# A two-layer graph network on one core: the mixers' output products folded, the second mixer moved between the edge tiles, the table stage reordered

## The reference, cut to what matters

```python
edge_index = jnp.stack([src, dst])
xn = _layernorm(x)
x = x + _L0_gnn_ref(xn, edge_index, ...) + _L0_mix_ref(xn[None], ...)[0]
x = x + _L0_ffn_ref(_layernorm(x)[None], ...)[0]          # top 2 of 8 experts
xn = _layernorm(x)
x = x + _L1_gnn_ref(xn, edge_attr_4, edge_attr_32, edge_index, ...) + _L1_mix_ref(xn[None], ...)[0]
x = x + _L1_ffn_ref(_layernorm(x)[None], ...)[0]          # one of 16 experts

def _L1_mix_ref(x, W_qkv, W_proj, b_proj):                # 8 heads of 64
    q, k, v = split(x @ W_qkv.T)
    q_, k_ = relu(q) + scale, relu(k) + scale
    kv, k_sum = einsum('bnhe,bnhf->bhef', k_, v), sum(k_, axis=nodes)
    z = 1.0 / (einsum('bnhe,bhe->bnh', q_, k_sum) + EPS)
    out = einsum('bnhe,bhef->bnhf', q_, kv) * z[..., None]
    return out.reshape(B, N, C) @ W_proj.T + b_proj

def _L1_gnn_ref(...):                                     # per edge e from node s to node d
    w = ssp(edge_attr @ W_f1) @ W_f2 * (ssp(s0(d, s) @ W_s1) @ W_s2)      # 512 weights of the edge
    edge_feat = w combined with x[s] and edge_sh          # 512 features
    out = segment_sum(edge_feat, edge_dst) + self_x       # then a linear map, + x
```

## Time and profile before

| | |
|---|---|
| profiled execution, its time | 5409.32 us |
| its span, first to last instruction | 5407.2 us |
| PE, DVE, POOL, ACT busy (share of the span) | 85%, 68%, 57%, 38% |
| mean granted TensorE clock | 0.922 of full speed |
| moved by DMA | 894.86 MB, mean 165 GB/s |

### The profile page before, as it was taken

How to read it: one execution, slowest core, us unless ns; L and a number is a source line. 1 busy time by engine, 2 the same in 40 slices (tenths; PEclk the granted TensorE clock), 3 DMA queues, 4 the chain that set the end, 5 groups by cost and what they waited for, 6 DMA issues and landing times. The chain is left out here.

```text
span 5407.2 us, 69046 instructions
## 1 busy us (share of the span) xinstructions
PE 4589.8 (85%) x17435; PEld 2475.2 (46%) x17436; DVE 3697.7 (68%) x9349; ACT 2077.3 (38%) x4487; POOL 3062.4 (57%) x2740
## 2 busy tenths in 40 slices
PE   6889988886999899597789888888888888888797
PEld 3346633232555555465556544443343343343463
DVE  6622279998999833324754488888888887878554
ACT  1112222222333211132300166666666666666310
POOL 0677767776777620123320288888888888888200
PEclk9999989998999999698899898899989998989898
DMA  4241157776666611644543499998888998988634
GB/s 148 77 145 44 44 168 210 210 210 166 193 196 194 187 40 52 228 129 139 176 156 129 148 202 205 203 206 200 201 202 199 204 203 195 203 199 200 162 104 144
DMA packets 363058, 894.86 MB, mean 165 GB/s; under 512 B 87037, under 2 KB 110188, under 8 KB 359205
## 3 DMA queue, kind: packets, MB, share of 16 engines
q0 software_dynamic: 212464, 648.99, 49.2%
q1 hardware_dynamic: 131151, 201.88, 11.1%
q10 hardware_dynamic: 19190, 41.03, 2.0%
HBM read 670.91 MB, written 221.22 MB: 165 GB/s over the span
## 5 line engine op out<-in xcount | busy, mean ns | idle before, releaser
L2028 POOL DMA_INDIRECT mid_acc<-m_out,m_il x416 | 703.8, 1692 | 142.1 <-issue 114.7
L2016 POOL DMA_INDIRECT m_drow<-mid_drow,m_ig x416 | 460.1, 1106 | 425.4 <-DMA m_ig<-in_dst_ix 290.1
L2240 PE MATMUL m_pws<-m_w,m_hid 32*128 32x512 f32 x832 | 499.8, 682 | 207.0 <-DVE m_hid L2070 180.0
L2248 PE MATMUL m_pm<-m_msg,m_same 128*128 128x512 f32 x832 | 528.3, 720 | 102.7 <-DVE m_msg L2107 64.2
L961 PE MATMUL m_pm<-m_vrow,m_same 128*128 128x512 f32 x880 | 513.5, 669 | 80.8 <-DVE m_vrow L904 79.5
L433 POOL DMA_INDIRECT mid_slots<-sort_rec,f_row x416 | 413.6, 994 | 246.5 <-issue 126.5
L888 POOL DMA_INDIRECT m_vrow<-mid_att_rows,m_ix x440 | 431.1, 980 | 167.9 <-PE m_pm L962 86.3
L2211 PEld LDWEIGHTS m_pip<-keep_ident,m_drow 128*128 128x128 f32 x2496 | 399.2, 219 | 255.3 <-issue 245.0
L2241 PE MATMUL m_pwf<-m_w,m_hid 32*128 32x512 f32 x832 | 507.4, 692 | 0.0
L735 POOL DMA_INDIRECT s_krow<-mid_att_rows,s_ix x440 | 416.0, 946 | 146.8 <-issue 123.1
L2016 POOL DMA_INDIRECT m_srow<-mid_srow,m_ig x416 | 425.9, 1024 | 126.8 <-issue 119.2
(11 more groups left out here) (386 smaller groups left out, 8981.0 us busy)
## 6 DMA issues: line engine op xcount, KB each, us to landing
x_line<-in_src_rows SPq DMA_DIRECT2D x26, 1024.0 KB, 5.2
mid_att_rows<-f_rows SPq DMA_DIRECT2D x75, 256.0 KB, 2.0
mid_ys<-e_y SPq DMA_DIRECT2D x57, 256.0 KB, 2.0
mid_acc<-e_zero ACTq DMA_DIRECT2D x26, 512.0 KB, 8.1
g_q<-mid_qT SPq DMA_DIRECT2D x50, 256.0 KB, 4.4
g_a<-mid_acc SPq DMA_DIRECT2D x50, 256.0 KB, 2.9
mid_srow<-t_srow SPq DMA_DIRECT2D x5, 2240.0 KB, 7.3
keep_w<-in_w SPq DMA_DIRECT2D x16, 512.0 KB, 8.9
```

Source lines behind the costliest of these rows:

```text
L2016: pool.indirect_dma_start(row, None, table, bass.IndirectOffsetOnAxis(ap=ig[:, k // EH, n, k % EH:k % EH + 1], axis=0),).then_inc(s_g[k % ...
L2028: pool.indirect_dma_start(io["acc1"][k % NACC], bass.IndirectOffsetOnAxis(ap=il[:, k // EH, k % EH:k % EH + 1], axis=0), out[:, k % R, :], ...
L2240: pe.matmul(pws[k % 2][:], hid[0:HID, par, cols], w_2[0:HID, :], start=True, stop=True)
L2248: pe.matmul(pm[:], same[:, k // B % 2, k % B, :], msg[:, k % 2, :], start=True, stop=True).then_inc(s_seg, 1)
```

## The change: what it does

- **Folded mixers.** In merge0 and merge1 kv is multiplied by the output weights once (kvw, 4 matmuls of 128x512 after a turn of kv). Per tile q is divided by its normalizer: ksum is now 128 columns wide, so that PE (`head_sums`) gives the normalizer of every column, ACT adds the epsilon (`normalizers`), VectorE takes the reciprocal of 128x512 and multiplies q by it, and PE multiplies q by kvw. The products with 2 columns, the turn of the result and ACT's copy of it are gone. In merge1 both output biases come in by a matmul with two rows (`two`, `extra`), and own rows are no longer loaded nor added.
- **front0.** keys and three of five member steps run ahead of the first tile; all later steps of the sort stand four places earlier. k'v and k'1 are one product with 129 columns.
- **load_consts, experts0.** One index table fewer is loaded, and the bf16 lines are no longer made. Only one accumulator and the last 128 rows of the other are cleared (14 DMAs for 26). The counts, with 52 broadcasts of 512 KB that GpSimd issues, and the lead rows are made in experts0.
- **tables1.** xT has two buffers; norms, turns and square sums of a pass stand in the middle of the pass before; ACT squares and adds the residual in place of VectorE and GpSimd; the hidden products stand ahead of the destination rows. srow's first part is stored from drow, and the node's own rows are stored to srow and once more to the accumulator acc1[0].
- **mixer1 and leads1 are gone.** In edges1 the blocks 1 to 25 each take one node tile of the mixer. The target numbers come as 512 KB broadcasts into SBUF instead of 4 KB rows and a matmul, and the ring of source rows has 12 slots.

```diff
@@ front0: order(k)
-                    if k == 0:
-                        keys()
-                    elif k < 1 + U:
-                        member(k - 1)
-                    elif k < 19:
-                        rank(2 * (k - 6))
+                    if k < 2:
+                        member(3 + k)
+                    elif k < 15:
+                        rank(2 * (k - 2))
...
-                    elif k == 22:
+                    elif k == 18:
                         bases(pcnt[:, 0:NT], pcnt[:, NT:2 * NT])
-                    elif 23 <= k < 23 + 2 * SORT_C:
+                    elif 19 <= k < 19 + 2 * SORT_C:
...
                 norms(0)
+                norms(1)
+                keys()
+                for a in range(3):
+                    member(a)
                 vec.wait_ge(s_bias, 16)
@@ merge0 (merge1 alike)
+                def divide_queries(i, j):
                     n = U * i + j
+                    vec.wait_ge(s_zq, n + 1)
+                    vec.reciprocal(zq[:, n % 2, :], zq[:, n % 2, :]).then_inc(s_rq, 1)
+                    vec.wait_ge(s_rq, n + 1)
+                    vec.tensor_tensor(q[:, j, :], q[:, j, :], zq[:, n % 2, :], ALU.mult).then_inc(s_q, 1)
...
+                for c in range(KC):
+                    need(pe, s_kvw, c - 1)
+                    pe.matmul(pk[c % 2][:], kvT[:, P * c:P * (c + 1)], w_out[:, c, :], start=True, stop=True).then_inc(s_kw, 1)
...
-                            pe.matmul(pout[j % 2][:], oT[:, j, P * c:P * (c + 1)], w_out[:, c, :], start=c == 0, stop=False)
+                            ins = pe.matmul(pout[n % 2][:], q[:, j, P * c:P * (c + 1)], kvw[:, c, :], start=False, stop=c == KC - 1)
@@ experts0: VectorE, with lines(b) on GpSimd for each half block
                 for n in range(XS + 2):
                     if n < XS:
                         first(n)
+                    if n < 2 * EB:
+                        counts(n, 0)
                     if n >= 2:
                         second(n - 2)
+                    if n < 2 * EB:
+                        counts(n, 1)
+                    if n == 2 * EB:
+                        vec.wait_ge(s_cnt, ET)
+                        lead_rows(vec, s_lead, keep.src, count, spare, go, leads)
@@ tables1: PE
+                turns(0)
...
                 for i in range(NB):
-                    body(i)
+                    scalars(i)
+                    hidden(i)
+                    destinations(i)
+                    gates(i)
+                    if i + 1 < NB:
+                        turns(i + 1)
+                    sources(i)
@@ edges1
-        S, R, B = EU, 4, 4
+        S, R, B = 12, 4, 4
...
-                        sp.dma_start(line[:, h, :], lines[:, cols]).then_inc(s_line[h], 16)
+                        mine = sources[(2 * b + h) * EH * P:(2 * b + h + 1) * EH * P].partition_broadcast(P)
+                        sp.dma_start(line[:, h].rearrange("p t n -> p (t n)"), mine).then_inc(s_line[h], 16)
+                        if h == 1:
+                            node(b)
...
+                def mixer(b, k):                       # PE, last in the body of edge tile k
...
+                    if k in (0, 1, 2, 3):
...
+                        for c in range(KC):
+                            ins = pe.matmul(px[:, P * k:P * (k + 1)], W[:, c, P * k:P * (k + 1)], xT[:, P * c:P * (c + 1)],
+                                            start=c == 0, stop=c == KC - 1)
+                    elif k in (5, 6, 7, 8):
...
+                        ins = pe.matmul(px[:], xT[:, P * c:P * (c + 1)], W[:, c, D:2 * D], start=c == 0, stop=c == KC - 1)
+                    elif k in (9, 10, 11, 12):
...
+                        ins = pe.matmul(px[:], xT[:, P * c:P * (c + 1)], W[:, c, 2 * D:3 * D], start=c == 0, stop=c == KC - 1)
+                    elif k == 14:
...
+                        for c in range(3):
+                            ins = pe.matmul(px[:, (P + 1) * c:(P + 1) * (c + 1)], key[:, P * c:P * (c + 1)], val[:, c, :],
+                                            start=True, stop=True)
+                    elif k == 15:
...
+                        ins = pe.matmul(px[:, 0:P + 1], key[:, 3 * P:D], val[:, 3, :], start=True, stop=True)
@@ program
-            run(mixer1)
-            run(leads1)
             run(edges1)
```

More of the change, by code:

```diff
@@ L1407, in experts0 @@
         zero = s.sb("zero", [P, 2 * D])
+        count, lower, spare = s.sb("count", [P, ET]), s.sb("lower", [P, P]), s.sb("spare", [P, 1])
+        line, junk = s.sb("line", [P, 2, EH, P], I32), s.sb("junk", [P, 2, P])
+        go, leads = s.sb("go", [P, 2, ET]), s.sb("leads", [P, ET], I32)
+        s_low, s_cnt, s_lead, s_lead_out = (s.sem(n) for n in ("lower", "counts", "lead_steps", "leads_out"))
+        s_line = [s.sem(f"line{k}") for k in range(2)]
         s_zero, s_z = s.sem("zero"), s.sem("sums_cleared")
@@ new lines, in norms, with residuals @@
+                def norms(i):
+                    act.wait_ge(s_sum, 2 * (i + 1))
+                    need(act, s_g1, 4 * i)
+                    act.activation(n1[:], sq[:, 0, :], ACT.Sqrt, scale=1.0 / 3.0).then_inc(s_n1, 1)
+                def residuals(i):
+                    act.wait_ge(s_v, NORM * (i + 1))
+                    for j in range(U):
+                        n = U * i + j
+                        act.wait_ge(s_xn, n + 1)
+                        act.activation(keep.X[:, n, :], keep.X[:, n, :], ACT.Identity, bias=resid[:, 1, n:n + 1],
+                                       scale=resid[:, 0, n:n + 1]).then_inc(s_res, 1)
@@ L2265, in body @@
                             inner(*there)
-                        if k % B == 0 and (there := at(b, k + B)):
-                            spread(*there)
                         if k % B == 1 and (there := at(b, k + 3)):
                             hidden(*there)
+                        mixer(b, k)
                 for b in range(EB):
@@ L2389, in _ @@
-                edges(0, 0)
-                mixed(0, 0)
-                pe.wait_ge(s_w, 48)
+                turn_kv(pe, keep.kv, keep.ident, pk[1]).then_inc(s_kv, 1)
+                sums(0, 0)
+                turn(0, 0)
+                pe.wait_ge(s_w, 64)
+                pe.wait_ge(s_two, 1)
+                pe.wait_ge(s_kvT, 1)
+                for c in range(KC):
+                    need(pe, s_kvw, c - 1)
+                    pe.matmul(pk[c % 2][:], kvT[:, P * c:P * (c + 1)], w_p[:, c, :], start=True, stop=True).then_inc(s_kw, 1)
```

830 lines of the change are left out of this document (399 added, 431 removed).

## The result

The changed kernel takes 5136.0 us (median of four runs, 5127.2 to 5150.2); beside it the kernel before took 5405.4. The ratio is 0.9508, with a 95% interval of 0.9493 to 0.9523. The forecast was 5012 in a range of 4965 to 5115: the direction was right, the time lies outside the range.

A forecast was written before the change was run, and what follows sets the result against it. GpSimd's issuing was taken to bound edges1. Terms −329.5 (mixer1, leads1), +32 (edges1), −19 (front0), −25 (merge0), −5 (merge1), −12 (experts0), −35 (tables1), −0.5 (load_consts) sum to −394: 5409.3 to 5015.3, less 3.6 gives 5012, range 4965 to 5115.

The forecast's parts named there:

- What bounds the kernel now: Reading of stage limits: edges1 is GpSimd's, 4.72 us per tile of issuing and gaps, times 416 = 1964 us.
- edges1, PE: PE has 68.3 us of full-clock work per block, 75.9 at 0.90, under GpSimd's 77.2; 31 us charged, bound +130.
- edges1, the ring: In edges1, 12 slots for 16 bind only when landings pass 12 us: cost nothing.
- edges1, DMA: In edges1, added mixer and line traffic of 129 us raises the DMA share from 0.89 to 0.94.
- +32: Whole edges1 term: 31 us for PE's narrow margin and 1 for the start; bounds −5 to +130.
- Rival 1: PE becomes the limit in edges1, +130 instead of +32: 5110 us; chance 0.17.
- rival 5: In edges1, VectorE's compare with two SBUF inputs stalls GpSimd, 110 us in all: 5122 at most; chance 0.03.
- front0: Stage front0: first scatter near 134 instead of 153.2, GpSimd's and PE's ends both earlier: −19 us, bounds 0 to −28.
- merge0: Stage merge0: 1.25 us less per tile on PE, about +5 for folding kv: −25 us, bounds −31 to +10.
- merge1: Stage merge1: tile from 6.95 to 6.57 us on PE, two-row bias product 0.87: −5 us, bounds −10 to +12.
- rival 6: Reciprocal of 512 columns takes 4.3 us or more, making merge1 VectorE's, +6 instead of −5: 5023 us; chance 0.08.
- experts0, tables1: experts0: 12 fewer clearing DMAs −15.4, counts' line loads +3, together −12 us; tables1: blocks near 31 us, −35 us.

The follow-up runs named there:

- no_products: Changed kernel without the mixer's arithmetic in edges1, its loads of xT, stores of q and the lines kept: 5169.5 us, edges1 2187.
- before_ring12: Kernel before with a ring of 12 source rows instead of 16 in edges1, nothing else: ratio to before 0.9998, edges1 2004.6 us against 2006.1.
- lines_once: Changed kernel with edges1's 512 KB target-number broadcasts issued for block 0 alone (2 of 52): 5036.4 us, edges1 2067.
- bare12: Changed kernel without the mixer's arithmetic, xT loads and q stores in edges1, lines for block 0 alone: edges1 2007.7 us, ratio to before 0.935.
- one_input: Changed kernel with each four-tile compare written as four instructions with one SBUF input and one number per partition: 5149.3 us, edges1 2184.
- line_pool: Changed kernel with edges1's 512 KB lines issued by GpSimd on its own queue instead of by SP: 5083.7 us, edges1 2118.
- before_lines_pool: Kernel before plus 52 unread 512 KB broadcasts in edges1, issued by GpSimd on its own queue: edges1 2082 us, ratio to before 1.012.

## Why the prediction was wrong, step by step

- **What bounds the kernel now**: right. edges1 was and stays GpSimd's; 0.30 us lie between its instructions as before. One row was misread on the way: the 290.1 us put down to an index load are not many gaps of 0.30 us but one wait of 290.1 us, ahead of the first gather and almost all of it before the stage. The sum of 4.72 us per tile doesn't use it.
- **edges1, PE**: the work was right. Forecast 68.3 us of full-clock work per block; 1893.0/26 × 0.92 = 67.0. But the 31 us charged for it measured nothing, and the +130 bound was built on PE as the limit: no_products excludes both.
- **edges1, the ring**: right (before_ring12).
- **edges1, DMA: the step that failed.** The prediction added SP's transfers to the mean share of the DMA engines, got 0.94 of the stage, and costed them at nothing as long as that stayed under 1. Their own size was right, 129 us per engine forecast and 134 measured. But it took GpSimd's 1.692, 1.106 and 1.024 us as fixed. They are not: they became 1.846, 1.164 and 1.155, and the share fell to 0.85 in a longer stage. The term "+32" measured +169: 108 lines, 59 xT and q (lines_once, bare12, no_products).
- **Rival 1** (PE) and **rival 5** (the shared port) were excluded by no_products and one_input; no rival had the mechanism that happened. Without it the sum is good: everything outside edges1 was forecast at −426 and came to −436 (5409.3 − 5141.95 is 267.4, and 169 were lost).
- **front0**: the first scatter starts at 132.2 (134 forecast), and the last ones follow each other by 1.26 us to the end, so GpSimd sets the stage's end as argued.
- **merge0**: −29.9, its mechanism right. **merge1**: a tile takes 6.90 us against 6.95, not 6.57, all of it on PE, which waits for nobody. The product with two rows costs nearly what the rest saved (1.05 for 1.10 us):

```profile
4838.49 1.05 PE L2460 MATMUL g_pout<-g_w_o,g_aT 128*128 128x128 f32 x8
4839.38 1.06 PE L978 MATMUL g_pn<-g_q,keep_ksum 128*128 128x128 f32 x8
4840.27 0.60 PE L2430 MATMUL g_tpa<-keep_ident,g_a 128*128 128x128 f32 x4
4840.80 1.12 PE L2451 MATMUL g_pout<-g_extra,g_two 2*128 2x512 f32 x2
4841.85 3.70 PE L2456 MATMUL g_pout<-g_kvw,g_q 128*128 128x512 f32 x8
4845.39 1.05 PE L2460 MATMUL g_pout<-g_w_o,g_aT 128*128 128x128 f32 x8
```

  From 4840.80 to 4841.85 the bias product takes 1.05 us, not 0.87, and what left the tile is 6.95 + 1.05 − 6.90 = 1.10 us, not 1.25.
- **The reciprocal** (rival 6): it was 3.35 us, nearer to the slope of the earlier trace rows (3.5) than to the 4.3 estimated from the Trainium skill, "VectorE: DVE Perf Modes", section "First, the fixed hardware budget". The measurement decides:

```profile
L2350 DVE RECIPROCAL g_zq<-g_zq 128x512 f32<-128x512 f32 x25 | 83.6, 3346 | 0.7 <-ACT g_zq L2392 0.7
```

- **experts0, tables1**: within 2 us (12 × 1.27 is 15.2, not the 15.4 of the sum). ACT's second copy waits 17.09 us instead of 32.95:

```profile
2204.32 0.60 ACT L1497 ACTIVATE e_xT<-e_tp 128x512 f32<-128x512 f32 x1 [17.09 <-issue]
```

## What to carry to other kernels

Where GpSimd's indirect DMAs set the pace, their issue times are not constants: transfers that SP issues lengthened them here at a mean DMA share of 0.85, though the engines were full for some 16 us after a load. The price was 4.1 to 4.5 us of stage per MB (108 us for 26 MB of lines, 59 for 13 MB of xT and q), and 6.0 in the kernel before (163 for 27 MB). Cost added transfers there by such a measured price, and try to issue them from GpSimd's list as well as making them smaller; on one chip either brought 56 to 60 us. And when a stage's limit is forecast with a thin margin on one engine, price the others' resources with the same care: the whole miss was in the term taken as zero.

## What the runs showed of the hardware that was not expected

- After a 512 KB load on SP's queue one or two of GpSimd's indirect DMA issues, mostly, take up to 2.9 us longer, 75 of 86 of them 12 to 24 us after it. GpSimd's queue then holds an ordinary number of packets when the long issue begins (median 146, over all instructions 174) and none when it ends. The long issues come in a few lengths (3.86 and 2.52 us often for the two gathers, 2.6 to 3.3 for the scatter), and the ten of the kernel before, which has no such load, have the same: the loads make them frequent. Issued by GpSimd itself, the same load adds 0.63 us to its chain and leaves fewer long issues (32 for 86, 8 for 88). The Trainium skill, "DMA: Bandwidth & Descriptors", section "SWDGE vs HWDGE vs iDMA", says that GpSimd's queue and those of SP and ACT are different queues inside each DMA engine, which takes from them in turn, and recommends SP or ACT for plain transfers. Nothing in line_pool and before_lines_pool contradicts the first; the advice cost 60 us in this stage. What GpSimd does in a long issue no trace here shows. That moving the load from SP's list to GpSimd's removes most of them is shown in two kernels; whether by the queue or by the moment of the issue stays open.
- PE's work fell by 165 us in no_products and its mean granted clock fell too, from 0.92 to 0.85.
- On some chips the same front0 took 1114 us instead of 671 (before_ring12), while edges1 took the same time. The work is not slower: PE is busy 623 us against 605. It stands still seven times, up to 79 us, ahead of the same turn, with nothing that the profile shows as its cause; why is open:

```profile
PE f_tpn L582 <- issue: 426.4, 7, 79.3
```
